# One program between two layers' attentions, and a mixture of experts run inside the last attention's steps

## The reference

```python
h = _ln(x) * (1 + sc_mca) + sh_mca
h = _topk_cross_attn(h, context, w_q, b_q, w_kv, b_kv, w_co, b_co)
x = x + h * g_mca
h = _ln(x) * (1 + sc_mlp) + sh_mlp
h = _swiglu(h, w_m1, b_m1, w_m2, b_m2)
x = x + h * g_mlp
...
nx = _layer_norm(x, ln_gamma, ln_beta)
...
evidence = jnp.einsum('btp,bph->bth', weights, v)
...
combined = jnp.concatenate([nx, evidence, anchor], axis=-1)
router_logits = combined @ router_W + router_b
router_probs = jax.nn.softmax(router_logits, axis=-1)
h = jax.nn.silu(jnp.einsum('btc,ecr->bter', combined, e_w1) + e_b1)
expert_out = jnp.einsum('bter,erh->bteh', h, e_w2) + e_b2
routed = jnp.sum(expert_out * router_probs[..., None], axis=-2)
g = jax.nn.sigmoid(jax.nn.silu(combined @ gate_w1 + gate_b1) @ gate_w2 + gate_b2)
refined_delta = g * (routed @ out_w + out_b)
return x + refined_delta
```

## Time and profile before

| | us |
|---|---|
| median of 3 runs | 4627.36 |
| fastest and slowest of the runs | 4610.62, 10193.9 |
| profiled execution, whole time | 4624.74 |
| its span | 4623.0 |
| TensorE's mean granted clock | 0.80 |

### The profile page before, as it was taken

How to read it: one execution, slowest core, us unless ns; L and a number is a source line. 1 busy time by engine, 2 the same in 40 slices (tenths; PEclk the granted TensorE clock), 3 DMA queues, 4 the chain that set the end, 5 groups by cost and what they waited for, 6 DMA issues and landing times. The chain is left out here.

```text
span 4623.0 us, 75349 instructions
## 1 busy us (share of the span) xinstructions
PE 3625.3 (78%) x28388; PEld 1609.1 (35%) x28388; DVE 3536.7 (77%) x5424; ACT 2945.9 (64%) x5480; POOL 691.4 (15%) x1464
## 2 busy tenths in 40 slices
PE   2769999976789999858367778787787878778877
PEld 2323333332323333323132334334343434334543
DVE  7658989826568888537699998898989889898213
ACT  1556888844647878627377776767677677766413
POOL 1322122004234242013011010000101000000000
PEclk7788999987879999878666677777777667766769
DMA  4553353205434333144311011110111011000000
GB/s 138 147 132 85 85 112 84 57 22 144 120 91 95 90 94 80 24 107 118 80 36 43 22 29 37 31 34 19 40 30 37 18 32 34 13 12 10 13 19 9
DMA packets 277795, 280.05 MB, mean 61 GB/s; under 512 B 38960, under 2 KB 252472, under 8 KB 276536
## 3 DMA queue, kind: packets, MB, share of 16 engines
q1 hardware_dynamic: 277432, 275.22, 23.9%
HBM read 149.53 MB, written 124.43 MB: 59 GB/s over the span
## 5 line engine op out<-in xcount | busy, mean ns | idle before, releaser
L1369 DVE TENSOR_REDUCE mpart<-ring 128x1 f32<-128x400 f32 (+2 forms) x2816 | 1293.0, 524 | 273.9 <-PE ring L1156 267.1
L1287 ACT ACTIVATE prob<-xa_ps 128x512 f32<-128x512 f32 (+1 forms) x2048 | 1109.8, 596 | 243.5 <-PE xa_ps L1201 223.1
L2068 ACT ACTIVATE prob<-x_ps 128x512 f32<-128x512 f32 (+1 forms) x832 | 451.9, 598 | 313.3 <-PE x_ps L1926 246.5
L1156 PE MATMUL ring<-k_st,q_st 52*128 52x400 bf16 (+2 forms) x2560 | 580.7, 340 | 43.2 <-DMA k_st<-k_dram 11.3
L1790 PE MATMUL ring<-k_st,q_st 52*128 52x400 bf16 (+1 forms) x1024 | 330.5, 444 | 294.2 <-ACT s_sb L2004 276.3
L1220 PE MATMUL xa_ps<-prob,va 128*9 128x256 f32 x6656 | 506.4, 383 | 0.4 <-ACT prob L1287 0.4
L2283 DVE MAX8 mpart<-s_sb 128x8 f32<-128x1601 f32 x256 | 456.1, 1817 | 61.5 <-ACT s_sb L2004 61.5
L2004 ACT ACTIVATE s_sb<-ring 128x400 f32<-128x400 f32 (+1 forms) x1024 | 468.2, 517 | 40.1 <-PE ring L1790 31.8
L1995 ACT ACTIVATE un<-s_sb 128x1601 fp8e4<-128x1601 f32 x256 | 392.9, 1536 | 128.8 <-DVE s_sb L2292 128.3
L2286 DVE MATCH_REPLACE8 s_sb<-mpart,s_sb 128x1601 f32<-128x1601 f32 x256 | 461.9, 1812 | 0.0
L2292 DVE MATCH_REPLACE8 s_sb<-m8b,s_sb 128x1601 f32<-128x1601 f32 x256 | 461.8, 1812 | 0.0
(11 more groups left out here) (291 smaller groups left out, 4195.3 us busy)
## 6 DMA issues: line engine op xcount, KB each, us to landing
k_st<-kc_dram SPq DMA_DIRECT2D x192, 300.2 KB, 5.5
o_dram<-o_sb SPq DMA_DIRECT2D x192, 128.0 KB, 1.8
kc_dram<-k SPq DMA_DIRECT2D x72, 300.0 KB, 3.4
ctx_t<-in_ctxT SPq DMA_DIRECT2D x24, 800.5 KB, 4.8
q_st<-q_dram SPq DMA_DIRECT2D x80, 192.0 KB, 4.2
kc_dram<-k SPq DMA_DIRECT2D x72, 200.0 KB, 3.9
k_st<-k_dram SPq DMA_DIRECT2D x48, 192.0 KB, 5.0
kc_dram<-k SPq DMA_DIRECT2D x24, 300.8 KB, 3.3
```

The source lines that it names most:

```text
L1156: nc.tensor.matmul(ring_ps[:, r % BANKS, 0:w], q_st[rows, b % NQ, 2 * t + pl, qt * P:(qt + 1) * P], k_st[rows, slot_of(n), pl, c0:c0 + w], ...
L1287: nc.scalar.activation(prob[0:size, s % NPROB, hf * 512:(hf + 1) * 512], x_ps[0:size, (2 * s + hf) % XBANKS, :], ACT.Exp, scale=HEAD_SCALE ...
L1369: nc.vector.tensor_reduce(mpart[:, n % 4, row, c:c + 1], ring_ps[:, r % BANKS, 0:chunks[c][1]], AX.X, ALU.max).then_inc(g["red"].sem, 1)
L2068: nc.scalar.activation(prob[0:size, s % NPROB, hf * 512:(hf + 1) * 512], x_ps[0:size, (2 * s + hf) % XBANKS, :], ACT.Exp, scale=HEAD_SCALE ...
```

## The change

Two parts. In the first, `stage_mlp`, the next layer's `stage_load` and its `stage_project` become one block, `stage_between`, run by the class `Between`. It goes by levels, each over the four chunks: output projection, mean, variance, diagonal, normalisation, modulation of the next layer, up, down; then mean, variance, diagonal, normalisation and projection of the next layer. Ahead of layer 0 only the second half runs. Four PSUM banks rotate, four more hold means and variances. The weights of the next layer that lie ahead of "co" and the vectors (now two sets) are loaded at the start of the block, the rest behind the last down matmul. The values are written straight into the tile from which the self attention reads them; their DRAM tensor is gone. q and k of batches 0 and 1 are loaded from DRAM (8 DMAs) inside the block, behind the chunk 0 stores, and the self attention begins without them. In layer 2 the mask rows are loaded at the block's start.

In the second part `stage_last` takes in the experts. Their weights go by one DMA into the tile that held the attention's keys, at step 417, and other tiles of the attention hold their intermediate results. Chunks 0, 1 and 2 stand at steps 426 to 440, 441 to 455 and 456 to 470, one use a step, each with its matmuls, its ACT part and its DVE part placed behind what the step already had; chunk 3 stands at steps 495 to 509, behind batch 7's result. Their four PSUM banks (`xa_ps`; seven, `ex_ring`, before) are those that scores and values of the attention had. The third `stage_load`, `stage_experts` and their barriers are gone.

```diff
-        self.v_dram = dram("v_dram", (B, P, 2, NH * VW), F32)
...
+    HEAD = ("op", "mean", "var", "diag", "norm", "mod", "up", "down")
+    TAIL = ("mean", "var", "diag", "norm", "proj")
...
+        self.by_pool = [("k", c) for c in range(NC - 1)]
+        self.by_dve = [("q", c) for c in range(NC)] + [("k", NC - 1)]
+        self.uses, self.at, self.nth, n = [], {}, {}, {"act": 0, "dve": 0}
...
+    def waves(self):
+        for k, m in self.levels:
+            for c in range(NC):
+                yield k, m, c
...
+        def bank_free(use):
+            u = self.at[use]
+            if u == 3 and self.layer is not None:
+                pe.wait_ge(s["bias"].sem, s["bias"].at(1))
+            if u >= 4:
+                old = self.uses[u - 4]
+                read = s[self.reader(old)]
+                pe.wait_ge(read.sem, read.at(self.nth[old]))
...
+            elif k == "mod" and c == 0:
+                pe.wait_ge(s["w"].sem, s["w"].at(32))
+                bank_free(("mod", 0))
+                act_in = p.cond if self.nxt == 1 else p.cact
+                for i in range(self.n_mod):
+                    last = nc.tensor.matmul(self.out(("mod", 0))[:, i * B:(i + 1) * B], weight(p, self.nxt, "mod", i), act_in[:], start=True, stop=True)
+                last.then_inc(s["mm"].sem, 1)
...
+            elif k == "down":
+                pe.wait_ge(s["act"].sem, s["act"].at(self.nth[("up", self.NF - 1), c]))
+                bank_free(("down", c))
+                for f in range(self.NF):
+                    last = nc.tensor.matmul(self.out(("down", c)), weight(p, self.layer, "m2", f), self.hid[:, c, f, :], start=f == 0, stop=f == self.NF - 1)
+                last.then_inc(s["mm"].sem, 1)
...
+                if m and c == 0:
+                    act.wait_ge(s["mod"].sem, s["mod"].at(1))
...
+    def sp(self, sp):
+        p, s, nxt = self.p, self.s, self.nxt
+        if self.layer is not None:
+            n_w, free = W_OFF[nxt][1], W_OFF[self.layer][0]["co"]
+            sp.dma_start(p.w[:, 0:free, :], p.io[f"w{nxt}"][:, 0:free, :]).then_inc(s["w"].sem, 16)
+            sp.dma_start(p.vec[:, nxt % 2, 0:V_OFF[nxt][1]], p.io[f"v{nxt}"]).then_inc(s["w"].sem, 16)
+        if self.rope:
...
+            sp.wait_ge(s["mm"].sem, s["mm"].at(self.at["down", NC - 1] + 1))
+            sp.dma_start(p.w[:, free:n_w, :], p.io[f"w{nxt}"][:, free:n_w, :]).then_inc(s["w2"].sem, 16)
...
+        for what, c in (("q", 0), ("k", 0), ("q", 1), ("k", 1), ("q", 2)):
+            store(what, c)
+        sp.wait_ge(s["st0"].sem, s["st0"].at(32 * len(RUNS)))
+        for b in range(Q_AHEAD):
+            load_queries(p, sp, self.q_self, b, s["loaded"])
+            load_keys(p, sp, b, s["loaded"])
+        for what, c in (("q", 3), ("k", 2), ("k", 3)):
+            store(what, c)
+        for name in ("loaded", "st", "w", "w2", "init"):
+            if self.totals[name]:
+                sp.wait_ge(s[name].sem, s[name].at(self.totals[name]))
...
+EXPERT_USES = [("r", e, "act") for e in range(N_EXP)]
+for expert in range(N_EXP):
+    EXPERT_USES += [("h", (expert, 0), "act"), ("h", (expert, 1), "act"), ("y", expert, "dve")]
+EXPERT_USES += [("g1", 0, "act"), ("g2", 0, "act"), ("o", 0, "dve")]
+N_EXPERT = len(EXPERT_USES)
...
-            self.end = d + 62
+            self.end = d + 59
+        self.experts, self.stores = {}, {}
+        self.weights = self.STEPS * B + 1
+        for c in range(NC):
+            at = self.STEPS * B + 10 + c * N_EXPERT if c < NC - 1 else self.end
+            for n in range(N_EXPERT):
+                self.put(self.experts, at + n, (c, n))
+            self.put(self.stores, at + N_EXPERT + 1, c)
+        self.end += N_EXPERT + 2
...
+        w_all = p.k_flat[:, 0:2 * W_OFF[3][1] * P].bitcast(F32).rearrange("p (n c) -> p n c", c=P)
+        w_e = lambda name, n=0: w_all[:, W_OFF[3][0][name] + n, :]
+        e_hid = un_flat[:, 0:4 * 2 * E * 2 * CH].bitcast(F32).rearrange("p (k e r c) -> p k e r c", k=2, e=E, r=2)
...
+                if k == order.weights:
+                    sp.wait_ge(g["x"].sem, g["x"].at(2 * END))
+                    sp.dma_start(w_all, p.io["w3"]).then_inc(x["w"].sem, 16)
...
+            def anchors():
+                pe.wait_ge(g["exp"].sem, g["exp"].at(2 * END))
+                pe.wait_ge(g["ocopy"].sem, g["ocopy"].at(NU))
+                pe.wait_ge(x["w"].sem, x["w"].at(32))
+                pe.wait_ge(x["rw"].sem, x["rw"].at(1))
...
+            def expert(c, n):
+                kind, i, _ = EXPERT_USES[n]
+                if n == 0:
+                    pe.wait_ge(g["h"].sem, g["h"].at(4 * c + 4))
+                    pe.wait_ge(g["ev"].sem, g["ev"].at(2 * c + 2))
+                before = e_bank(c, n) - EBANKS
+                if before == 0:
+                    pe.wait_ge(x["an"].sem, x["an"].at(1))
+                elif before > 0:
+                    old_c, old_n = divmod(before - 1, N_EXPERT)
+                    read = EXPERT_USES[old_n][2]
+                    pe.wait_ge(x[read].sem, x[read].at(e_nth(read, old_c, old_n)))
...
+                for c, n in order.experts.get(k, []):
+                    if (c, n) == (0, 0):
+                        anchors()
+                    expert(c, n)
...
+                for c, n in order.experts.get(k, []):
+                    expert_out(c, n)
+                    if EXPERT_USES[n][1] == (0, 0):
+                        expert_exp(c)
...
+            def expert_begin():
+                dve.wait_ge(g["t16"].sem, g["t16"].at(NU * HQ))
+                dve.wait_ge(g["chain"].sem, g["chain"].at(8 * NPAIR))
+                dve.wait_ge(g["av"].sem, g["av"].at(END))
+                dve.wait_ge(x["w"].sem, x["w"].at(16))
+                at = V_OFF[3][0]["rw"]
+                nc.vector.tensor_copy(e_rw, p.vec[:, 1, at:at + 9][:, :, None].to_broadcast([P, 9, P])).then_inc(x["rw"].sem, 1)
```

More of the change, by code:

```diff
@@ new lines, in _ @@
+            sp.wait_ge(loaded.sem, loaded.at(16 * n_dma))
+        @block.gpsimd
+        def _(pool):
+            for hf in range(2):
+                nc.gpsimd.memset(p.q_st[64 * hf + 32:64 * hf + 64], 0.0).then_inc(rows_set.sem, 1)
+            pool.wait_ge(rows_set.sem, rows_set.at(2))
+        @block.scalar
+        def _(act):
+            act.wait_ge(loaded.sem, loaded.at(16 * n_dma))
+            nc.scalar.activation(p.cact[:], p.cond[:], ACT.Silu).then_inc(act_ready.sem, 1)
+        @block.tensor
@@ new lines, in dve @@
+        done = 0
+        for k, m, c in self.waves():
+            cols = slice(c * CH, (c + 1) * CH)
+            n = NC * m + c
+            if k in ("op", "down"):
+                self.residual(dve, c, k)
+            elif k == "mean":
+                dve.wait_ge(s["mean"].sem, s["mean"].at(n + 1))
+                nc.vector.tensor_tensor(self.h[:, c, :], p.x[:, cols], self.stat[:, c, :], ALU.subtract).then_inc(s["xc"].sem, 1)
+            elif k == "var":
+                dve.wait_ge(s["var"].sem, s["var"].at(n + 1))
+                nc.vector.tensor_scalar(self.rv[:, c, :], self.stat[:, c, 0:4], EPS[self.norms[m][0]], None, ALU.add).then_inc(s["rv"].sem, 1)
+                dve.wait_ge(s["rv"].sem, s["rv"].at(2 * n + 1))
+                nc.vector.reciprocal(self.rv[:, c, :], self.rv[:, c, :]).then_inc(s["rv"].sem, 1)
+            elif k == "diag":
+                dve.wait_ge(s["rstd"].sem, s["rstd"].at(n + 1))
+                nc.vector.tensor_tensor(self.f[:, c, :].rearrange("p (k m) -> p k m", k=4), p.const[:, C_ID, :][:, None, :].to_broadcast([P, 4, P]),
+                                        self.rstd[:, c, :][:, :, None].to_broadcast([P, 4, P]), ALU.mult).then_inc(s["diag"].sem, 1)
+            elif k == "norm":
+                dve.wait_ge(s["bc"].sem, s["bc"].at(n + 1))
+                dve.wait_ge(s["sq"].sem, s["sq"].at(n + 1))
+                nc.vector.tensor_tensor(self.h[:, c, :], self.h[:, c, :], self.stat[:, c, :], ALU.mult).then_inc(s["xn"].sem, 1)
+            elif k == "mod" and c == 0:
+                self.modulation(dve)
+            elif k == "proj" and c == 0:
+                for what, chunk in self.by_dve:
+                    done = self.split(dve, nc.vector, s["dchain"], done, what, chunk, s["dparts"])
@@ L557, in _ @@
-            for g in range(NV):
-                m = NI * stepn + g
-                if g < 3:
-                    pe.wait_ge(pf.sem, pf.at(m - 2))
-                else:
-                    pe.wait_ge(v_out.sem, v_out.at(g - 2))
-                for k in range(4):
-                    last = nc.tensor.matmul(pp[:, m % 3, k * P:(k + 1) * P], norm.h[:, g, k * P:(k + 1) * P], weight(p, layer, "v"), start=True, stop=True)
-                last.then_inc(v_mm.sem, 1)
+            bt.pe(pe)
         @block.scalar
@@ L627, in stage_project @@
-    pf.passed(NI * stepn)
-    for name, mine in turn.items():
-        chain[name].passed(len(mine) * (PER - 1))
-        parts[name].passed(len(mine))
-    stored.passed(16 * len(RUNS) * NI)
-    norm.done()
```

(11 more changed lines are left out.)

1013 lines of the change are left out of this document (434 added, 579 removed).

## The result

| | us |
|---|---|
| median before, 3 runs | 4627.36 |
| median after, 3 runs (4508.28 to 4523.71) | 4512.63 |
| ratio, 95% interval | 0.9755 (0.972 to 0.979) |
| profiled execution before, span | 4623.0 |
| profiled execution after, span | 4506.5 |

The change takes 115 us away in the medians and 116.5 in the two spans; the sum of the forecast was 104.9. Four places of the new trace tell where, one for each term of the sum.

The account below looks back on a forecast made before the run. No engine is full; gains lie in the seams between layers and at the end. Seams −57, end −118.7, copy +1.4, experts beside the chain +69.4 make −104.9: 4520 us, forecast 4500 to 4534, range 4488 to 4570.

Parts of the forecast that it names:

- A: Seams between cross attention and next self attention, fronts plus tails: −57 us, bounds −62 and −43.
- the front: Output projection to next projections in two seams: gains 19.6 and 21, sum 41 us; 28 with both bounds wrong.
- the tail: First store of q to first score, ahead of layers 0, 1, 2: gains 1.5, 3.8, 10.7, together 16 us.
- The mixture: Chunks 0 to 2 of the experts in the chain's steps 426 to 470: +69.4 us, bounds +52 and +87.
- the copy: A DVE copy, the old L2424, now at step 417: +1.4 us at most, 0 if hidden.
- Rival 1: Steps 426 to 470: expert chunks do not overlap the chain; 36 us more, 4556 us; chance 0.12.
- Rival 2 and 5: Steps 426 on: clock only 0.70, +36, 4556 us, chance 0.13; or staying at 0.50, 4633 us, chance 0.04.
- Rival 3: ScalarE's table loads among steps 426 to 470 all lie on the path: +31 us, 4551 us; chance 0.07.
- Rival 4: Seam tails: the stores' order gains nothing, as loads stand ahead of three stores: +16 us, 4536 us; chance 0.09.
- Behind batch 7: From batch 7's result to the end, only chunk 3 left: 45.1 us in place of 163.8, −118.7.
- Long attention stages that change, which I count at nothing: Sign that the forecast is wrong: long attention stages change, though no instruction in them moved; counted at nothing.

Follow-up runs that it names:

- the changed kernel's second execution: The changed kernel measured again, unaltered, on one chip beside two further versions: 4514.7 us.
- the second part alone: Changed kernel's `stage_last`, with experts in the last attention's steps, behind the seams of the kernel before: 4584.7 us, ratio 0.990.
- the kernel without overlap: Changed kernel with all four expert chunks placed behind batch 7's result, none beside the chain: 4552.9 us, ratio 0.983.
- chunk 2 moved: Changed kernel with chunk 2 moved from steps 456-470 to 474-488, beside batch 7's x3 matmuls: 4502.9 us, ratio 0.972; again 4508.8 us.

## Why the prediction was right

**What bounds the kernel.** That seams and end were the places, and that the gain would be their sum, held: 105.0 of the 116.5 us between the two spans are in these terms, for which the sum had 104.9. That it came so near is partly luck: single terms were off by up to 3.4 us, on both sides. The bound of −43 for A does not follow from its own terms (28 for the front and 0 for the tail give −28); the measured −51.6 lies inside both.

**Front of the seams.** Forecast 63.3 us to the first projection, measured 63.8; the modulation 1.40 us as taken (1.4), ups and downs 27.7 against 27.5, last down to projection 13.2 as taken. The 63.7 that the second seam's sum starts from should be the 63.3 of the first; 65.0 was measured. One reason was wrong: the text put the smooth ups and downs down to four rotating banks. With three the same block needs 28.2, so the fourth bank gives 0.5 of the 4.7 us.

**Tail.** The DMA sum (26.7 + 2.3) gave 29.0 ahead of layers 2 and 0; 29.7 and 30.5 were measured. Over all traces with the order of the change both lie between 29.3 and 30.6, so the two do not differ and the sum was about 1 us low for both. Ahead of layer 0, where 30.5 became 30.5, nearly nothing was to be won. Ahead of layer 1 the forecast had SP held by k1 until 1072.5 − 1054.2 = 18.3 us behind the first store; in the new trace q2 goes out 1054.16 − 1034.90 = 19.3 us behind it, and the gain was 2.2 in place of 3.8. That the loads would be late next if they were moved past the three last stores was right: so placed they cost 3.1 us more there.

**The mixture.** +69.4 and 1.4 for the copy forecast, +68.8 measured. For steps 426 to 470 the forecast had 142.6 us, 125 of them busy and 17.6 idle at a clock of 0.90; the trace has 143.5, 126.6 and 16.9 at 0.92. That the middle of the two bounds for the idle time was right is luck: no row led to it. Two small things are missing in its sum: the anchors' 20 matmuls, 4.3 us at the head of the mixture (4279.72 to 4284.0), and some 2.7 us of x3, since a window of 29.00 us stood for the 31.7 of the first ten steps. Rival 1 (no overlap, +36) is refuted by the kernel that has none: 37.3 us slower. Rival 2 and 5 (clock) by the rows. Rival 3 (table loads on the path, +31) is worth 6.2 for 16 loads; the stretch has 18 more than before, in place of 24. Rival 4 by the tails, 12.1 us less in all.

**Behind batch 7.** 45.1 was forecast from the end of batch 7's result, with 1 us for four banks and 2.8 for the store; it was 4506.5 − 4464.8 = 41.7, with none for the banks, a chunk of 4464.92 to 4503.37 + 0.69, 39.1 (41.0 taken), and 2.4 behind it. The first chunk from a low clock took 1.9 us less than the one of before, and 1.5 of that lie in one place: TensorE waits some 5 us for the Silu ahead of y0, and the clock is low behind the wait for longer in the kernel before (first two rows) than in the changed one (last two):

```profile
4490.48 3.78 PE L2382 MATMUL ex_ring<-ex_hid,w 128*128 128x512 f32 x4 [5.13 <-ACT ex_hid L2415]
4494.06 1.91 PE L2382 MATMUL ex_ring<-nx,w 128*128 128x512 f32 x2
...
4481.43 3.54 PE L1984 MATMUL xa_ps<-un,k_st 128*128 128x512 f32 x4 [4.69 <-ACT un L2149]
4484.81 1.02 PE L1984 MATMUL xa_ps<-nx,k_st 128*128 128x512 f32 x2
```

**What no step foresaw.** "Long attention stages that change, which I count at nothing" is the item that was off: 11.5 us. By what the traces show it is not the change's doing. 8.7 of the 11.5 lie in the long attention of layer 2: from its first block mark to its last exponent it took 2075.2 us before and 2066.5 after. The same instructions took 2077.0 in the changed kernel's second execution and 2058.6 with the second part alone, and between 2058.6 and 2078.6 in the thirteen traces. The windows of these four, in this order:

```profile
2247.60:4322.80 2075.20, 1577.54 (x10963) 770.46 (x10964) 1870.67 (x1709) 1447.80 (x2510) 139.24 (x312) 0.71 0.11 27
2193.10:4259.60 2066.50, 1565.22 (x10964) 762.54 (x10965) 1870.03 (x1709) 1448.24 (x2510) 139.77 (x312) 0.71 0.11 27
2197.90:4274.90 2077.00, 1577.52 (x10964) 768.71 (x10965) 1870.30 (x1709) 1447.76 (x2510) 139.38 (x312) 0.71 0.11 27
2281.60:4340.20 2058.60, 1555.14 (x10964) 759.41 (x10965) 1869.97 (x1709) 1447.46 (x2510) 139.36 (x312) 0.72 0.11 28
```

VectorE and ScalarE are busy for the same time to within 1 us; TensorE's time differs by 22 us, and the stage is longer where TensorE is busy for longer. Over pieces of 100 us its granted clock differs from one execution to the next (between 0.64 and 0.73 in the second piece). Ahead of this stage the scatter is as wide: layer 2's last self attention exponent lies at 2139.3 us in the kernel without overlap and at 2162.3 in the one with chunk 2 moved, on one chip and with the same instructions up to there. The 11.5 us are inside that scatter.

## What to carry to other kernels

TensorE shown 100% busy at a granted clock of 0.50 is a place with room, not a full one: lay work with long matmuls beside it and read the clock again. Take the price between two instructions that stand in both kernels: 24 us of matmuls cost 12 here. Where a stage boundary shows a hole, ask first which transfer starts in it; moved to the front of the stage, its cost was gone here, and the meeting of the engines alone was small. Measure a move in a stretch between two instructions that both kernels have: it repeated to 0.1 us for the changed kernel's last stage (204.7 or 204.8 in six traces) and to 3 us for the version with chunk 2 moved (194.0, 190.9), where whole runs scattered by 25.

## What the runs showed of the hardware

Short fp32 matmuls with hardly a gap between them (42.05 of 43.0 us busy) did not raise the granted clock from 0.50, that is 1.2 GHz; with 512-column matmuls among them it stood at 0.97 and the same 256-column pair took 0.59 us in place of 1.20. What it is in the added matmuls that brings the clock up, no run separates.
The Trainium skill ("TensorE: Matmul & The Clock Gate", What's actually happening) says that the default state is throttled and activity releases it. These traces agree where the clock rises within a chunk, and show 43.0 us with TensorE busy for 42.05 in which it was not released. The Trainium skill ("TensorE: Matmul & The Clock Gate", A second HAM failure mode: psum-queue depth-cycling) tells of a clock that flips where a kernel cycles through PSUM banks; with four rotating banks the mixture stood at 0.92 in the mean, and once the clock was up the lowest window of 15 us showed 0.77 (4345 to 4360, TensorE busy for 9.5 us).

Two executions of one program can differ by 25 us, and the mean granted clock goes with it: on one chip the changed kernel took 4500.0 and 4505.7 us at 0.811 and 0.812, and 4523.6 and 4525.5 at 0.802. Between its two traces (spans 4506.5 and 4521.8) the difference lies ahead of the last exponent, 15.3 us, and none of it in the 204.8 and 42.1 behind. Whether the clock is the cause or follows from something else no run shows.
